# Routed sweep of a recurrent layer with experts: tokens turned by VectorE and SBUF transfers in place of TensorE's transposes

## What is computed

```python
xn = layernorm(x)                                  # 8192 tokens of 512
s = recurrence(xn, W1, b1, W2, b2, init_h)         # a gated recurrence over the sequence, in log space
shared = swiglu(xn, shared_gate, shared_up, shared_down)
e = argmax(xn @ gate_w)                            # one of 32 experts for each token
xs = xn * sigmoid(max(xn @ gate_w))
routed = (silu(xs @ gate[e]) * (xs @ up[e])) @ down[e]     # 512 -> 1024 -> 512, by token
out = x + s * silu(shared + routed)
```

## Time and profile before

| | |
|---|---|
| median of three runs | 3934.16 us (3931.18 to 3934.38) |
| profiled execution, its own time | 3924.13 us |
| its span | 3922.4 us |
| TensorE, VectorE, ScalarE, GpSimd busy | 98%, 53%, 51%, 18% of the span |
| routed sweep | from about 2590 us to the end |
| its mean granted clock | 0.993 |

### The profile page before, as it was taken

The page is one execution under the profiler, slowest core; times in us unless marked ns, Lnnn a source line. Parts: engine busy times, 40 slices in busy tenths (PEclk is TensorE's granted clock), DMA queues, the critical chain, the costliest instruction groups (busy, mean ns, idle before and its releaser), DMA issues.

```text
span 3922.4 us, 57778 instructions
## 1 busy us (share of the span) xinstructions
PE 3840.2 (98%) x19582; PEld 3292.4 (84%) x19583; DVE 2094.7 (53%) x3234; ACT 2012.2 (51%) x2860; POOL 720.5 (18%) x840
## 2 busy tenths in 40 slices
PE   8999999999989999999999999989999999999998
PEld 6888888888867788888888888879999999999997
DVE  5232322323246755555555555566667767677675
ACT  4222222222227667676767767765555546565553
POOL 2011010110105200000000000014323334343333
PEclk9999999999989999999999999999999999999999
DMA  5122121121121111000000100056676867777683
GB/s 177 61 78 83 64 86 64 78 83 59 78 57 44 42 68 39 32 32 32 32 32 32 62 34 32 22 198 232 215 241 230 276 215 258 249 271 252 215 276 124
DMA packets 273544, 466.41 MB, mean 119 GB/s; under 512 B 25402, under 2 KB 172987, under 8 KB 269636
## 3 DMA queue, kind: packets, MB, share of 16 engines
q1 hardware_dynamic: 235860, 346.48, 25.6%
q0 software_dynamic: 37616, 119.08, 8.8%
HBM read 364.73 MB, written 102.99 MB: 119 GB/s over the span
## 4 chain that ended last, share of the span: by engine, by line
PE 58%; DVE 4%; issue 3%; ACT 3%; DMA 2%; DVEq 1%; SPq 0%; POOL 0%; ACTq 0%; POOLq 0%
PE bank L87 13%; PE bank L88 13%; PE bank L89 13%; PE bank L1732 9%; PE bank L1108 5%; PE bank L1112 3%; DMA raw<-in_L_ffn_routed_down_w 1%; PE bank L1682 1%; DVE wlo L1378 1%; DVE yo L1630 1%; DVE hs L988 1%; DVEq L1251 1%; ACT L955 0%; DVE th L1612 0%; DMA harmless<-in_L_attn_x,at_x 0%
## 5 line engine op out<-in xcount | busy, mean ns | idle before, releaser
L87 PE MATMUL bank<-txT,whi 128*128 128x256 f32 (+2 forms) x2048 | 614.6, 300 | 11.5 <-DVE th L1612 5.6
L89 PE MATMUL bank<-txT,wlo 128*128 128x256 f32 (+2 forms) x2048 | 610.1, 298 | 0.0
L88 PE MATMUL bank<-txT,whi 128*128 128x256 f32 (+2 forms) x2048 | 610.1, 298 | 0.0
L87 PE MATMUL bank<-xT,w_hi 128*128 128x512 f32 x1536 | 599.6, 390 | 2.5 <-DVE b2all L1013 2.5
L88 PE MATMUL bank<-xT,w_hi 128*128 128x512 f32 x1536 | 599.1, 390 | 0.0
L89 PE MATMUL bank<-xT,w_lo 128*128 128x512 f32 x1536 | 598.8, 390 | 0.0
L1378 DVE TENSOR_TENSOR wlo<-raw,whi 128x1024 fp32r<-128x1024 f32 x372 | 445.7, 1220 | 45.2 <-ACT whi L1373 44.7
L548 DVE TENSOR_TENSOR h_act<-h_act,psU 128x512 f32<-128x512 f32 x128 | 88.0, 688 | 689.1 <-PE psU L89 686.7
L1732 PE MATMUL bank<-whi,thT 128*128 128x512 f32 x1264 | 409.8, 395 | 3.7 <-DVE thT L1616 2.1
L1373 ACT ACTIVATE whi<-raw 128x1024 fp32r<-128x1024 f32 x372 | 384.1, 1050 | 40.1 <-DMA raw<-in_L_ffn_routed_down_w 23.8
L87 PEld LDWEIGHTS bank<-txT,whi 128*128 128x128 f32 x2048 | 390.9, 191 | 16.2 <-DVE th L1612 8.2
(11 more groups left out here) (207 smaller groups left out, 7642.9 us busy)
## 6 DMA issues: line engine op xcount, KB each, us to landing
raw<-in_L_ffn_routed_gate_w SPq DMA_DIRECT2D x124, 512.0 KB, 3.8
raw<-in_L_ffn_routed_up_w SPq DMA_DIRECT2D x124, 512.0 KB, 5.4
raw<-in_L_ffn_routed_down_w SPq DMA_DIRECT2D x124, 512.0 KB, 5.9
xT_dram<-xT SPq DMA_DIRECT2D x16, 2048.0 KB, 6.3
xT<-xT_dram SPq DMA_DIRECT2D x14, 2048.0 KB, 8.1
xs_dram<-x_in SPq DMA_DIRECT2D x16, 1024.0 KB, 4.4
ss_dram<-y_sb SPq DMA_DIRECT2D x64, 256.0 KB, 2.0
ss_dram<-ry SPq DMA_DIRECT2D x64, 256.0 KB, 2.1
```

The costliest lines, as they stand in the source:

```text
L87: pe.matmul(out, w[0], x[0], start=start, stop=False)
L88: pe.matmul(out, w[0], x[1], start=False, stop=False)
L89: return pe.matmul(out, w[1], x[0], start=False, stop=stop)
```

## The change

In all pieces but the first, TensorE no longer turns the tokens. VectorE turns each group by 32 by 32 blocks (`turn`, after blocks 2, 4 and 6) from `xg[g]` into one buffer `blocks`; SyncE moves the 16 rectangles of blocks back into `xg[g]` with 16 transfers inside SBUF, each of 32 partitions by 512 bytes (`quarters`); `x_hi` and `x_lo` read the tokens from `xg[g]` through a rearranged view. The turn of a group waits until the transfers of the group before have landed. SyncE's order is now by pieces: the three `quarters` of the next piece stand between the loads of parts 3, 4 and 5. GpSimd gathers two pieces ahead: the tokens of p + 2 are fetched after `targets` of piece p, when the splits of piece p + 1 are done.

```diff
+        blocks = place("turned_blocks", [P, D], 196)
+        def tokens_of(p, g):
+            if isinstance(p, int) and p == 0:
+                return first_turned(g)
+            return xg[g][:].rearrange("p (r k j) -> p k r j", r=KD, k=KD)
+        def xT_of(p, a, g):
+            cols = xT[:, a, :, g * P:(g + 1) * P]
+            return cols if isinstance(p, int) and p == 0 else cols.rearrange("p k (r j) -> p k r j", r=KD)
...
@@ sync
-            with sp.Fori(2, E) as e:
-                for q in range(PARTS):
-                    if q < RING:
-                        sp.wait_ge(wlo_done[q + RING], 2 * e)
-                    else:
-                        sp.wait_ge(wlo_done[q - RING], 2 * e + 2)
-                    load_part(sp, q, e)
+            def quarters(p, g):
+                sp.wait_ge(blocks_turned, (p - 1) * GROUPS + g + 1)
+                for a in range(KD):
+                    for r in range(KD):
+                        sp.dma_start(xg[g][a * 32:(a + 1) * 32, r * P:(r + 1) * P],
+                                     blocks[r * 32:(r + 1) * 32, a * P:(a + 1) * P]).then_inc(quarters_landed[g], 16)
+            def second(q, e):
+                sp.wait_ge(wlo_done[q - RING], 2 * e + 2)
...
+                load_part(sp, q, e)
...
+            def last(p, e):
+                first = isinstance(e, int) and e == 0
+                if first:
+                    whole(p)
+                for n in range(RING):
+                    if not first:
+                        quarters(p + 1, n)
+                    if not (isinstance(e, int) and e == E - 1):
+                        second(RING + n, e + 1)
+                if not (isinstance(e, int) and e >= E - 2):
+                    for q in range(RING):
+                        sp.wait_ge(wlo_done[q + RING], 2 * e + 4)
+                        settle(sp, settled)
+                        load_part(sp, q, e + 2)
...
@@ gpsimd
-            def gathers(p, u, nxt):
+            def tokens(p, u):
                 for g in range(GROUPS):
-                    pool.wait_ge(xg_loaded[g], (p + 1) * 16)
+                    pool.wait_ge(xg_loaded[g], p * 16)
                 settle(pool, settled)
-                pool.tensor_copy(at_x[:], gather_at[:, bass.ds(nxt, WIDE)]).then_inc(at_x_done, 1)
-                pool.wait_ge(at_x_done, p + 2)
-                pool.wait_ge(turned_x, (p + 1) * GROUPS)
+                pool.tensor_copy(at_x[:], gather_at[:, bass.ds(u, WIDE)]).then_inc(at_x_done, 1)
+                pool.wait_ge(at_x_done, p + 1)
+                pool.wait_ge(xlo, p * GROUPS)
...
-                gathers(p + full, at, unit(u + full * SIZE + n))
+                gathers(p + full, at)
                 targets(p + full, at, third + full)
+                if not (isinstance(e, int) and e == E - 1):
+                    tokens(p + full + 2, unit(u + full * SIZE + n + size_of(p + full + 1)))
                 scatters(p + full, n)
...
@@ scalar
-                act.wait_ge(turned_x, p * GROUPS + g + 1)
+                    act.wait_ge(quarters_landed[g], p * 16 * KD * KD)
...
@@ vector
+            def turn(p, g):
+                dve.wait_ge(xg_loaded[g], (p + 1) * 16)
+                if g == 0:
+                    dve.wait_ge(xhi, p * GROUPS)
+                else:
+                    dve.wait_ge(quarters_landed[g - 1], p * 16 * KD * KD)
+                dve.transpose(blocks[:].rearrange("p (a k i) -> p a k i", a=KD, k=KD), by_block_row(xg[g][:]))\
+                    .then_inc(blocks_turned, 1)
...
                         lo(b // 2 - 1, (b % 2,))
+                    if b in (2, 4, 6):
+                        turn(p + 1, b // 2 - 1)
...
@@ tensor
-            def turn_x(p, g):
...
-                    if b == NI - 2:
-                        turn_x(p + 1, 0)
...
-                    turn_x(p + 1, 1)
...
-                    third(pe, ahead, lambda: turn_x(p + 1, 2), lambda: passed_x(p + 1, 2))
```

More of the change, by code:

```diff
@@ L1228, in recurrent_and_routed @@
         turned_x = k.sem("turned_x")
+        blocks_turned = k.sem("blocks_turned")
+        quarters_landed = [k.sem(f"quarters_landed{g}") for g in range(GROUPS)]
         xhi = k.sem("txhi")
@@ L1306, in first_turned, with by_block_row @@
         def first_turned(g):
-            return (psX, by_block(psG[1]), by_block(psU[0]))[g]
-        def bank_x(p, g):
-            return first_turned(g) if isinstance(p, int) and p == 0 else psX
+            return by_bank(banks[(0, 2, 3)[g]])
+        def by_block_row(row):
+            return row.rearrange("p (k a i) -> p a k i", k=KD, a=KD)
+        def tokens_of(p, g):
[5 more added lines that the diff above has]
+            return cols if isinstance(p, int) and p == 0 else cols.rearrange("p k (r j) -> p k r j", r=KD)
         def raw_of(q, e):
@@ new lines, in second, with whole @@
+            def second(q, e):
+                sp.wait_ge(wlo_done[q - RING], 2 * e + 2)
+                if isinstance(e, int) and e == 1:
+                    sp.wait_ge(whi_done[q], 2)
+                settle(sp, settled)
+                load_part(sp, q, e)
+            def whole(p):
+                for g in range(GROUPS):
+                    quarters(p + 1, g)
+            def last(p, e):
[8 more added lines that the diff above has]
+                if not (isinstance(e, int) and e >= E - 2):
+                    for q in range(RING):
+                        sp.wait_ge(wlo_done[q + RING], 2 * e + 4)
+                        settle(sp, settled)
+                        load_part(sp, q, e + 2)
@@ new lines, in expert @@
+            def expert(e):
+                p = order(sp, FIRST_PIECE, e, 0, E + MOST)
+                full = order(sp, FULL, e, 0, MOST)
+                settle(sp, settled)
+                with sp.If(full > 0):
+                    with sp.Fori(0, MOST) as i:
+                        with sp.If(full > i):
+                            whole(p + i)
+                last(p + full, e)
+            expert(0)
+            with sp.Fori(1, E - 2) as e:
+                expert(e)
+            expert(E - 2)
@@ L1413, in gathers, with size_of @@
                     fetch(xg[g][:], xs_dram, index(at_x, g), xg_loaded[g])
+            def size_of(p):
+                p = nc.s_assert_within(p, 0, E + MOST, skip_runtime_bounds_check_because="there is such a piece")
+                return pool.value_load(listed[0:1, 1, bass.ds(p, 1)], min_val=LEAST, max_val=MOST_UNITS)
+            def gathers(p, u):
                 for done, count in stored:
@@ L1472, in expert @@
                 return p + full + 1, third + full, n
+            tokens(1, unit(size_of(0)))
             with pool.Fori(0, E - 1) as e:
```

22 lines of the change are left out of this document (10 added, 12 removed).

## The result

The changed kernel takes 4388.53 us (median of four runs, 4386.77 to 4391.61) against 3932.67 (four runs, 3930.42 to 3934.38) for the kernel before in the same comparison: 1.116 times as long, 95% interval 1.1141 to 1.118. The sign was as predicted, the size was not: 4074 was forecast, and 4388 lies outside the range of 3955 to 4210.

What follows compares the result with a forecast made beforehand. TensorE was taken to bound every piece. Chained transfers would add 17 x 8.5 + 13 x 0.8 - 2 x 1.3 = +152 us, less 12: +140 on 3924.1, 4064; the median 10 above gives 4074 us, range 3955 to 4210.

Steps and rivals of the forecast that it cites:

- I take 0.40 with the gap, between the lone store and the row of four: SyncE's sixteen transfers a group: 0.40 us an issue, between 0.33 for a lone store and 0.46 to 0.48; 6.4 us for sixteen.
- the upper bound of 0.48: SyncE's dearest issue, from four loads of `places`: 0.48 us each, giving small pieces of 47.0 us and 4182 us in all.
- link: SyncE's time from a group turned to its sixteen transfers landed: 8.1 us, three times a piece, strictly one after another.
- the 12 us taken off for the first and last piece: In the sum of +152 us: the first piece already waits for loads, the last has no successor; leaves +140 us.
- The loop: In-order VectorE, from one third `x_lo` to the next: 9.3 + 6.3 + 26.4 + 1.4 = 43.4 us against 34.9 in a small piece.
- A large piece keeps its 51.1 less 1.3: The two large pieces of the sweep: not held up by the transfers, each 1.3 us shorter without TensorE's transposes.
- The landing: The last of a group's transfers lands 2.0 us after its issue, as the 256 KB stores do.
- 35 us of TensorE: TensorE's 80 groups of transposes at 0.44 us, all on the path: removing them alone would give 3889 us.
- The covers: SyncE's delayed weight loads and GpSimd's later gathers stay hidden; D1, just hidden by the stretched piece, up to 2 us late.
- The other moves: SyncE's new order of weight loads and GpSimd's later gathers: hidden; order loads and `If`s some tenths while SyncE waits anyway.
- Cheap issues: Rival at SyncE's sixteen transfers: perhaps 0.1 us an issue, TensorE bounds again, 3904 us; decides below about 0.19 us; chance 0.12.
- The fallen clock: Rival: idle TensorE's clock falls, first turn and all behind it 4 to 5 us later, up to +85 us, 4160; chance 0.15.

Runs made afterwards that it cites:

- the sixteen from DRAM: The changed kernel with each group's sixteen transfers read from fixed rows of xs in DRAM instead of from blocks in SBUF: 4177.96 us, 1.0642 to the kernel before.

## Why the prediction was wrong in size and right in kind

- **The step that failed** is the term "I take 0.40 with the gap, between the lone store and the row of four". Sixteen issues took 10.04 us, 0.63 each, and the upper bound of 0.48 fell too. Both bounds came from transfers with one end in DRAM; the change's have both in SBUF, and the sixteen from DRAM showed that this is the difference: 0.47 against 0.63. Even for those 0.47 was right and 0.40 was not: the nearest rows, 32 rows in a row, were at hand, and I went below them towards a lone issue. The upper bound was also not the dearest row of the trace before. These four loads of 192 KB, 128 rows in three parts of 512 bytes each, come from DRAM and hold SyncE for 0.66 us each:

```profile
1154.29 2.66 SPq L858 DMA_DIRECT2D ry<-in_L_attn_W  x4
```

They are no nearer in kind, so they do not give the 0.63, but as the upper bound they give a link of 12.0 us and small pieces of 17.0 + 3 x 12.7 = 55.1, above the 53.1 to 54.1 measured. In the sum: 3 x 16 x 0.23 = 11.0 us a piece, less 3 x 0.46 because the tail behind the sixteenth issue was shorter (1.2 us, not 1.7), is 53.0 - 43.4 = 9.6 in a small and in a middle piece. 30 x 9.6 and 2 x 6.7 for the large ones are 301 of the 314 us by which the forecast fell short; the 12 us taken off for the first and last piece, which the difference of the spans doesn't show, are nearly the rest.
- **The loop was right**, term by term, in the small piece's loop above: 9.7 us to `th` of block 0 (9.3 forecast), 6.2 to turn 0 (6.3), 0.71 a turn (0.69), three links, 1.3 for the last splits (1.4). Middle pieces did lose less than small ones. The prediction took the piece's own size to set the loop; it is that of the piece whose totals are in it, and since each piece's totals stand in one loop the sum is the same. "A large piece keeps its 51.1 less 1.3" was false at this price, which makes the large ones a member of the chain as well.
- **The landing** of 2.0 us was 1.8, the reads of tokens 0.618 and 0.684.
- **35 us of TensorE, "all on the path"**: true of the middle and large pieces, but for the first middle one. With one issue a group 17 us of the 35 were missing, 9 of them in the small pieces, where VectorE seems to take them back, and 4 in the first middle piece. The prediction saw "how little room VectorE has" and charged it 5 us in the cheap case.
- **The covers held.** The other moves were free on their own (0.999), and in the sweep ScalarE waited twice for a weight part, 3.6 and 1.6 us: the stretched pieces hid D1 as foreseen.
- **Cheap issues** stays false by more than thought: the break-even was 0.19 us, the lone issue costs 0.52. The Trainium skill (DMA: Bandwidth & Descriptors, "Anatomy of one DMA") has some 50 ns for the sequencer's dispatch, but as one part of a transfer that GpSimd issues, and the prediction took it for the whole time for which SyncE is held. No run here shows that part by itself. For the whole time the traces decide, and the shortest issue of the earlier trace rows is 0.29 us.
- **The fallen clock** is there, 0.90 over the sweep against 1.00 before (the 0.993 in the table ahead is the mean of the whole execution), and it isn't the price. The loops above with a clock of 0.85 and 0.90 end within 0.4 us of a sum that holds no term for it. Turn 0 was to start 4 to 5 us later by it; in those two loops it starts 15.8 and 15.9 us after the loop does, where the sum has 15.6.

## What to carry to other kernels

Count the issues before the bytes: a transfer of 16 KB inside SBUF held its engine for 0.6 us, as one of 4 KB and one of 64 KB did, so 48 of them make 30 us a piece, and handing half to an engine that computes moves the bill into the path. Take an issue's price from rows that have the same kind of ends and the same number back to back, and where there is no such row, let the upper bound be at least the dearest row of the trace. Where a cross-partition move is what makes a cheap operation dear, see if the load ahead of it can place the data instead: four gathers of quarter rows did what sixteen transfers were for.

## What the runs showed of the hardware that was not expected

- An issue on SyncE with both ends in SBUF takes 0.52 us alone and 0.59 (0.63 from start to start) in a row, for 32 or 128 rows, 128 or 512 bytes each, and with or without a change of partitions. With DRAM as the source the same rectangle takes 0.42 (0.47 from start to start). That is no price of DRAM as such: the loads of 128 rows in three parts each, above, take 0.62 in the middle of the cases. Why the second end in SBUF makes it dearer stays open.
- SyncE and ScalarE issue side by side and hardly slow each other: eight each in 5.3 and 5.0 us, where eight of SyncE's at 0.63 would be 5.0.
- In the change a transfer of 16 KB lands after 1.8 us in the middle of the cases and 3.8 at most; with one a group, 3 us after weight loads were issued, after 2.9 and up to 7.7. The stores of 256 KB to DRAM took 4.6 to 8.7 us beside two loads of weights, 2.0 to 3.6 without.
- GpSimd's operations on 128x12 integers took from 0.21 to 2.65 us right behind gathers of its own; what makes the difference was not tested.
